# Dense stages of a graph layer: norms applied a tile later, a residual add moved to VectorE, two loads swapped, M1's first transposes before the last products

## The chip, the cores and the metric

One core of a Trainium2 chip runs the kernel. The metric is the device time of one execution in microseconds (us). Before the change the median of 3 runs is 567.51 us (563.29 to 567.92).

## The reference

A graph layer over 1250 nodes of width 512 and 20000 edges, float32 throughout:

```python
h = relu(layernorm(x))                                  # node_feats
msg = relu(h[src] + (edge_attr @ W_edge + b_edge))
aggr = segment_sum(msg, dst)
t = (1 + eps) * h + aggr
t = gelu(layer_norm(t @ W1 + b1, g1, be1))              # 512 -> 1024
t = gelu(layer_norm(t @ W2 + b2, g2, be2))              # 1024 -> 512
t = layer_norm(h + t, gA, bA)                           # "layer A"
m = gelu(t @ M1) @ M2
out = x + layer_norm(t + m, gB, bB)
```

## The kernel before

The edge part (gather, messages, scatter by one-hot products) fills some 300 us; the change does not touch it. It leaves `acc`, ten tiles of 128 nodes (NT = 10). The dense part follows. Every operand of a product is split into a high and a low float32r part, and each product is three matmuls of 128x512 (low by high, high by low, high by high), lines L1129 to L1131.

- **Stage 0** (s = 0, W1): per tile 4 transposes of the input tile on TensorE into `ps_t`, `lhs_high` (ScalarE copy, L739) and `lhs_low` (VectorE subtraction, L1001), then 24 matmuls into `ps_u`, then norm 1 and Gelu into `mid`.
- **Stage 1** (s = 1, W2): per tile 8 transposes, the same split, 24 matmuls, norm 2, Gelu, the residual row `res` (x, normalized again by ScalarE, L773) added on GpSimd (L545), and layer A's norm into `acc`.
- **M1 and M2**: `turn(2, ...)` transposes pairs of `acc` tiles (L1249), `inner(b, f, k)` is one of 8 blocks of M1's product for a batch of 4, 2 or 4 tiles (12 matmuls), `inner_values` on ScalarE applies Gelu twice (full and high part), `inner_low` on VectorE makes the low part, and `down` is M2's product.

The order is written out by hand, one program for each engine, with semaphores between them; each engine takes its instructions in order. In both stages TensorE's `step` does product(i) and then the transposes of tile i + 2. `after(s, i, p)` is the step of the other engines for tile i, whose buffers are picked by p = i mod 2. A normalization is: bias and sum (`add_product`, L1027), two tiny VectorE operations on the sum (L1030, L1031), a sum of squares on ScalarE (`variance`, L755), var + eps and its power -0.5 on GpSimd (`inv_std`, L532 and L534), then two VectorE passes: centre times gain (L1016) and scale plus shift (L1022). Layer A uses VectorE's batch-norm statistics instead (L1006, L1010) and centres in L1019. VectorE's step does it all for its own tile in one go: read the product, make the low part of tile i + 2, centre, wait for `rstd`, scale. In stage 1 it also does layer A of tile i - 1. The next weight matrix is loaded chunk by chunk in the steps of tiles 0 to 7 (`w_raw`), and split by ScalarE (`weight_high`, L750) and GpSimd (`weight_low`, L539).

TensorE reads the product buffers in turn: product(i) waits until VectorE has read product(i - 2) (`product_read`) and has made the low part of tile i (`lhs_lo_done`). In `step(1, 8)` the transposes of `acc` tiles 0 to 3 (`turn(2, 0)` and `turn(2, 1)`) come after product(1, 8); the first `inner` waits for the low parts of both. On SyncE, `load_tile(s, i + 2)` and `load_extras(s, i)` follow each other for each tile.

## Time and profile before

| | |
|---|---|
| median of 3 runs | 567.51 us (563.29 to 567.92) |
| the profiled execution | 562.67 us, of which its span 560.8 us |
| granted TensorE clock, mean of the span | 0.957 |
| busy in the span | TensorE 471.7, VectorE 407.6, ScalarE 300.4, GpSimd 325.4 us |
| W1 and W2 (stages 0 and 1) | about 301 to 437 us |
| M1 and M2 | 439 us to the end |

Busy shares are means over parts with different limits, so the stages have to be read one by one: on each engine's timeline, from the same operation of one tile to that of the next. A matmul row's duration includes its pipeline; the start-to-start distance tells the rate. A bracket at a row's end is the idle time before it and what ended it.

### The profile page before, as it was taken

Reading aid. Unit: us, or ns where it says so; the run is one execution under the profiler, and the core shown is the slowest. Engines: PE = TensorE matmul, PEld = TensorE weight load, DVE = VectorE, ACT = ScalarE, POOL = GpSimd, SP = SyncE. Lnnn points to the kernel's source line nnn. Section 1 sums busy time; section 2 is a strip of 40 time slices with the busy share of each in tenths; the row PEclk is TensorE's granted clock in tenths of the full one; section 3 lists DMA queues with packets and bytes.
Section 4 is the critical chain, followed back from the end, with each engine's and each line's share of the span. In section 5 each row is a group of like instructions: output and inputs, shape, how many; then the busy total and the mean of one; then the engine's idle time right before and its main releaser. Section 6 shows DMA issues by size and latency. Waiting matters only on the chain.

```text
span 560.8 us, 7864 instructions
## 1 busy us (share of the span) xinstructions
PE 471.7 (84%) x1915; PEld 348.7 (62%) x1916; DVE 407.6 (73%) x550; ACT 300.4 (54%) x569; POOL 325.4 (58%) x306
## 2 busy tenths in 40 slices
PE   1072999989679898898867999999998699999994
PEld 0041666656346565465546887778877589888883
DVE  7852999887379696688892888879999844472465
ACT  3742787786186786878881544455554555014000
POOL 4675788887588778888830444427777542240152
PEclk9997899989789899899989999999999799999998
DMA  8677567677667766669404522244442031121022
GB/s 279 240 210 225 181 200 233 206 220 212 192 198 209 212 203 205 193 201 348 125 1 176 207 79 79 116 151 128 148 136 76 0 97 55 39 85 29 21 92 75
DMA packets 31416, 85.26 MB, mean 152 GB/s; under 512 B 4592, under 2 KB 4928, under 8 KB 31360
## 3 DMA queue, kind: packets, MB, share of 16 engines
q0 software_dynamic: 12560, 41.17, 24.9%
q1 hardware_dynamic: 17984, 42.74, 22.2%
q10 hardware_dynamic: 816, 0.77, 0.5%
q8 instruction: 15, 0.25, 0.2%
q14 instruction: 41, 0.34, 0.2%
HBM read 72.07 MB, written 5.24 MB: 138 GB/s over the span
## 4 chain that ended last, share of the span: by engine, by line
PE 39%; DVE 24%; issue 19%; ACT 8%; POOL 4%; ACTq 3%; DMA 2%; DVEq 1%; another core or an unknown queue 1%; POOLq 0%
PE ps_t L1155 5%; DVE msg_lo L953 5%; DVE work L1022 5%; PE ps_u L1131 5%; PE ps_u L1129 5%; PE ps_u L1130 5%; PE ps_u L1139 4%; DVE z L948 4%; PE ps_t L1130 4%; PE ps_t L1131 4%; PE ps_t L1129 4%; POOL rstd L534 3%; ACTq L297 2%; ACT squares L755 2%; PE ps_t L1139 2%
## 5 line engine op out<-in xcount | busy, mean ns | idle before, releaser
L521 POOL DMA_INDIRECT rows<-gather_table,src_idx x157 | 190.6, 1214 | 60.4 <-issue 42.4
L697 ACT ACTIVATE msg_hi<-z 128x1024 fp32r<-128x1024 f32 (+1 forms) x79 | 82.8, 1048 | 67.7 <-DVE z L948 42.4
L953 DVE SCALAR_TENSOR_TENSOR msg_lo<-z,msg_hi 128x1024 fp32r<-128x1024 f32 (+1 forms) x79 | 100.8, 1277 | 0.7 <-ACT msg_hi L697 0.7
L1139 PE MATMUL ps_u<-we_raw,attr_raw 128*128 128x512 f32 x104 | 58.7, 648 | 39.7 <-issue 24.4
L532 POOL TENSOR_TENSOR var_eps<-mv,eps_t 128x1 f32<-128x1 f32 x40 | 11.5, 289 | 133.4 <-DVE mv L1010 68.4
L948 DVE TENSOR_TENSOR z<-ps_u,rows 128x1024 f32<-128x1024 f32 (+1 forms) x53 | 64.1, 1209 | 32.0 <-issue 14.7
L1129 PE MATMUL ps_u<-w_hi,lhs_lo 128*128 128x512 f32 x160 | 64.7, 405 | 4.2 <-DVE lhs_lo L1001 3.0
L1131 PE MATMUL ps_u<-w_hi,lhs_hi 128*128 128x512 f32 x160 | 62.9, 393 | 0.0
L1130 PE MATMUL ps_u<-w_lo,lhs_hi 128*128 128x512 f32 x160 | 62.8, 392 | 0.0
L1155 PE MATMUL ps_t<-msg_lo,onehot 128*128 128x512 f32 x145 | 60.7, 419 | 0.0
L1155 PE MATMUL ps_t<-msg_hi,onehot 128*128 128x512 f32 x145 | 57.7, 398 | 0.0
L1139 PEld LDWEIGHTS ps_u<-we_raw,attr_raw 128*128 128x128 f32 x104 | 20.4, 205 | 50.5 <-issue 30.5
L628 ACT ACTIVATE apart<-iota,neg_rel_last 128x128 f32<-128x128 f32 x160 | 50.6, 387 | 0.0
L1129 PE MATMUL ps_u<-we_hi,attr_lo 128*128 128x512 f32 x53 | 44.4, 837 | 0.0
L534 POOL TENSOR_TENSOR rstd<-var_eps,minus_half 128x1 f32<-128x1 f32 x40 | 40.3, 1007 | 3.1
L948 DVE TENSOR_TENSOR z<-ps_t,rows 128x1024 f32<-128x1024 f32 x26 | 31.7, 1219 | 11.7 <-PE ps_u L1131 7.1
L539 POOL TENSOR_TENSOR w_lo<-w_raw,w_hi 128x512 f32 (+1 forms) x24 | 34.6, 1444 | 8.6 <-ACT w_hi L750 8.6
L1129 PE MATMUL ps_u<-ff_in_hi,w_lo 128*128 128x512 f32 (+1 forms) x96 | 35.2, 366 | 5.0 <-DVE ff_in_lo L997 5.0
L786 ACT ACTIVATE ff_full<-ps_u 128x512 f32<-128x512 f32 (+1 forms) x24 | 12.7, 528 | 47.7 <-PE ps_u L1131 43.6
L1129 PEld LDWEIGHTS ps_u<-w_hi,lhs_lo 128*128 128x128 f32 x160 | 30.1, 188 | 11.7 <-issue 3.3
L1079 DVE TENSOR_TENSOR ff_lo<-ff_full,ff_hi 128x512 fp32r<-128x512 f32 (+2 forms) x24 | 14.7, 614 | 29.0 <-ACT ff_hi L787 29.0
L1130 PE MATMUL ps_u<-ff_in_lo,w_hi 128*128 128x512 f32 (+1 forms) x96 | 35.1, 365 | 0.0
(158 smaller groups left out, 1056.9 us busy)
## 6 DMA issues: line engine op xcount, KB each, us to landing
attr_raw<-in_attr_t SPq DMA_DIRECT2D x20, 512.0 KB
w_raw<-in_W SPq DMA_DIRECT2D x24, 256.0 KB, 2.7
tile_in<-mid SPq DMA_DIRECT2D x10, 512.0 KB, 3.3
res<-in_x SPq DMA_DIRECT2D x20, 256.0 KB, 2.7
xin<-in_x SPq DMA_DIRECT2D x5, 512.0 KB, 7.4
gather_table<-tab SPq DMA_DIRECT2D x5, 512.0 KB, 2.8
out<-work SPq DMA_DIRECT2D x10, 256.0 KB, 2.1
rows<-gather_table,src_idx POOLq DMA_INDIRECT x157
```

The costliest lines, as they stand in the source:

```text
L521: g.indirect_dma_start(rows[:, group.r, e % TPG, :], None, gather_table[:, :], bass.IndirectOffsetOnAxis(src_idx[:, e:e + 1].bitcast(u32), ...
L534: g.tensor_tensor(rstd[:, slot:slot + 1], var_eps[:, slot:slot + 1], minus_half[:, 0:1], ALU.pow).then_inc(LN[ln]["rstd"], 1)
L539: g.tensor_tensor(w_lo[1 - s % 2][:, cols], w_raw[:, p, :], w_hi[1 - s % 2][:, cols].bitcast(f32), ALU.subtract).then_inc(w_lo_done, 1)
L628: last = a.activation(apart[:, e, :], iota[:, 0:P], ACT.Square, bias=neg_rel_last[:, ds(g.gr * TPG + e, 1)])
L697: a.activation(pair(msg_hi, g, p), summed(g, p), ACT.Relu).then_inc(msg_hi_done, 1)
L948: v.tensor_tensor(summed(g, p), embedded(g, p), rows[:, g.r, 2 * p:2 * p + g.in_pair(p), :].rearrange("p a d -> p (a d)"), ALU.add).then_i ...
L953: v.scalar_tensor_tensor(pair(msg_lo, g, p), summed(g, p), 0.0, pair(msg_hi, g, p).bitcast(f32), ALU.max, ALU.subtract).then_inc(msg_lo_do ...
L1129: t.matmul(o, lhs[1][cols], rhs[0][rcols], start=first, stop=False)
L1130: t.matmul(o, lhs[0][cols], rhs[1][rcols], start=False, stop=False)
L1131: return t.matmul(o, lhs[0][cols], rhs[0][rcols], start=False, stop=last)
L1139: t.matmul(o[:, D:2 * D], attr_raw[:, g.k, (2 * p + 1) * P:(2 * p + 2) * P], we_raw[:, :], start=True, stop=True)
L1155: last = t.matmul(summed_in(bank), selection[:, e, :], m[:, g.r, e * D:(e + 1) * D], start=False, stop=(e == end and m is msg_hi), skip_gr ...
```

## The change

In stages 0 and 1 each VectorE step reads its product first and then applies the norm of the tile before it; ScalarE's Gelus move a tile later with it. Layer A's residual add goes from GpSimd to VectorE (`add_residual`), with the sum taken in the same instruction; its squares are summed on ScalarE; its norm is applied two tiles behind. GpSimd's `weight_low` waits for the norm of the tile before. SyncE sends the weight chunk ahead of the residual rows. TensorE does `turn(2, 0)` before product(1, 8) and `turn(2, 1)` before product(1, 9), and the splits of both are in step 8 of the other engines. The buffers of sums and means grow from 2 to 4 columns. The norm after M2 (layer B) keeps its code.

```diff
--- before.py
+++ after.py
@@ -432,6 +432,11 @@
             def load_extras(s, i, p):
+                if s < 3 and not (isinstance(i, int) and i >= CHUNKS):
+                    if not early(s, i):
+                        sp.wait_ge(w_lo_done, W1_CHUNKS + CHUNKS * s + i - 1)
+                    sp.dma_start(w_raw[:, p, :], A["W"][:, ds((s + 1) * WCOLS + i * D, D)]).then_inc(w_in[p], 16)
                 if s in (1, 3):
                     if not zero(i, 1):
...
                     elif s == 3:
                         sp.wait_ge(res_added, NT - 1 + i)
                     sp.dma_start(res[p][:, :], A["x"][ds(i * P, P), :]).then_inc(res_in[p], 16)
-                if s < 3 and not (isinstance(i, int) and i >= CHUNKS):
-                    if not early(s, i):
-                        sp.wait_ge(w_lo_done, W1_CHUNKS + CHUNKS * s + i - 1)
-                    sp.dma_start(w_raw[:, p, :], A["W"][:, ds((s + 1) * WCOLS + i * D, D)]).then_inc(w_in[p], 16)
@@ -528,39 +528,40 @@
             def inv_std(ln, i, slot):
-                pool.wait_ge(LN[ln]["squared" if ln in "12" else "moments"], i + 1)
+                pool.wait_ge(LN[ln]["squared" if ln in "12A" else "moments"], i + 1)
...
             def weight_low(s, i, p):
+                if s < 2 and not zero(i):
+                    pool.wait_ge(LN["12"[s]]["done"], i)
                 pool.wait_ge(w_hi_done, W1_CHUNKS + CHUNKS * s + i + 1)
...
-            def add_input(s, i, p):
-                if s == 1:
-                    pool.wait_ge(gelu2_ready, i + 1)
-                    g.tensor_tensor(work[p][:, D:H], work[p][:, D:H], res[p][:, :], ALU.add).then_inc(res_added, 1)
+            def shift_input(i, p):
...
+            def after(s, i, p):
+                weights = not (isinstance(i, int) and i >= CHUNKS)
+                if s == 0:
+                    inv_std("1", i, p)
+                    if weights:
+                        weight_low(0, i, p)
+                elif s == 1:
+                    if not zero(i, 1):
+                        inv_std("A", i - 2, 2 + p)
+                    if weights:
+                        weight_low(1, i, p)
+                    inv_std("2", i, p)
                 else:
...
-            def after(s, i, p):
-                if s < 2:
-                    inv_std("12"[s], i, p)
-                    if s == 1:
-                        if not zero(i):
-                            inv_std("A", i - 1, 3 - p)
-                        add_input(s, i, p)
-                    if not (isinstance(i, int) and i >= CHUNKS):
-                        weight_low(s, i, p)
-                else:
-                    add_input(s, i, p)
+                    shift_input(i, p)
                     inv_std("B", i, p)
...
                 if s == 1:
-                    inv_std("A", NT - 1, 3)
+                    for p in range(2):
+                        inv_std("A", NT - 2 + p, 2 + p)
...
@@ -749,30 +751,55 @@
...
-            def variance(ln, i, p, width):
+            def variance(ln, i, slot, x, width):
                 act.wait_ge(LN[ln]["mean"], i + 1)
-                a.activation(squares[:, 0:width], work[p][:, 0:width], ACT.Square, bias=neg_shift[:, p:p + 1],
-                             scale=float(width) ** -0.5, accum_out=mv[:, p, 1:2]).then_inc(LN[ln]["squared"], 1)
+                if not zero(i):
+                    act.wait_ge(LN[ln]["squared"], i)
+                elif ln != "1":
+                    act.wait_ge(LN["1"]["squared"], NT)
+                first = D if ln == "A" else 0
+                a.activation(squares[:, first:first + width], x, ACT.Square, bias=neg_shift[:, slot:slot + 1],
+                             scale=float(width) ** -0.5, accum_out=mv[:, slot, 1:2]).then_inc(LN[ln]["squared"], 1)
+            def gelu1(i, p):
+                act.wait_ge(LN["1"]["done"], i + 1)
+                a.activation(tile(mid, i), work[p][:, :], ACT.Gelu).then_inc(up_ready, 1)
+            def gelu2(i, p):
+                act.wait_ge(LN["2"]["done"], i + 1)
+                a.activation(work[p][:, D:H], work[p][:, 0:D], ACT.Gelu).then_inc(gelu2_ready, 1)
+            def input_rows(i, p):
...
+                a.activation(res[p][:, :], res[p][:, :], ACT.Relu, bias=x_nbias[:, ds(i, 1)], scale=x_rstd[:, ds(i, 1)])
             def after(s, i, p):
                 s2, i2 = ahead(s, i, p)
-                lhs_high(s2, i2, p)
-                variance("12"[s], i, p, H if s == 0 else D)
-                if not (isinstance(i, int) and i >= CHUNKS):
+                weights = not (isinstance(i, int) and i >= CHUNKS)
+                if s2 < 2 or i2 == 0:
+                    lhs_high(s2, i2, p)
+                if s == 1 and weights:
                     weight_high(s, i, p)
+                variance("12"[s], i, p, work[p][:, 0:H if s == 0 else D], H if s == 0 else D)
+                if s2 == 2 and i2 == 0:
+                    lhs_high(2, 1, 1)
                 if s == 0:
-                    act.wait_ge(LN["1"]["done"], i + 1)
-                    a.activation(tile(mid, i), work[p][:, :], ACT.Gelu).then_inc(up_ready, 1)
+                    if weights:
+                        weight_high(s, i, p)
+                    if not zero(i):
+                        gelu1(i - 1, 1 - p)
                 else:
-                    if isinstance(i, int):
-                        act.wait_ge(res_in[p], 16 * (i // 2 + 1))
+                    input_rows(i, p)
+                    if zero(i):
+                        gelu1(NT - 1, 1)
...
-                    act.wait_ge(LN["2"]["done"], i + 1)
-                    a.activation(work[p][:, D:H], work[p][:, 0:D], ACT.Gelu).then_inc(gelu2_ready, 1)
+                        gelu2(i - 1, 1 - p)
+                        variance("A", i - 1, 3 - p, work[1 - p][:, D:H], D)
@@ -787,6 +814,8 @@
...
                     weight_high(2, f, f % 2)
+                if b == 0 and f == 0:
+                    variance("A", NT - 1, 3, work[1][:, D:H], D)
...
@@ -798,6 +827,7 @@
...
                     after(s, NT - 2 + p, p)
+            gelu2(NT - 1, 1)
             lhs_high(2, 2, 0)
             inner_parts(act, 0, inner_values)
@@ -1021,56 +1051,71 @@
...
             def add_product(s, i, p, other, width):
                 dve.wait_ge(product_done, NT * s + i + 1)
                 v.scalar_tensor_tensor(work[p][:, 0:width], ps_u[p][:, 0:width], 1.0, other, ALU.mult, ALU.add,
                                        accum_out=total[:, p:p + 1]).then_inc(product_read, 1)
                 dve.wait_ge(product_read, NT * s + i + 1)
-                v.tensor_scalar(neg_shift[:, p:p + 1], total[:, p:p + 1], -float(width) ** -1.5, None, ALU.mult)
-                v.tensor_scalar(neg_mean[:, p:p + 1], total[:, p:p + 1], -1.0 / width, None, ALU.mult).then_inc(LN["12"[s]]["mean"], 1)
-            def layer_a(i, p, part):
+                mean("12"[s], p, width)
+            def norm1(i, p):
+                if zero(i):
+                    for name in ("g1", "be1"):
+                        dve.wait_ge(vec1_in[name], 16)
+                normalize("1", i, p, work[p][:, :], g1, be1, work[p][:, :]).then_inc(LN["1"]["done"], 1)
+            def norm2(i, p):
+                x = work[p][:, 0:D]
+                normalize("2", i, p, x, g2, be2, x).then_inc(LN["2"]["done"], 1)
+            def add_residual(i, p):
                 x = work[p][:, D:H]
-                if part == 0:
-                    dve.wait_ge(res_added, i + 1)
-                    moments("A", i, 2 + p, x, D)
-                else:
-                    normalize("A", i, 2 + p, x, gA, bA, tile(acc, i)).then_inc(h_ready, 1)
+                dve.wait_ge(gelu2_ready, i + 1)
+                v.scalar_tensor_tensor(x, x, 1.0, res[p][:, :], ALU.mult, ALU.add, accum_out=total[:, 2 + p:3 + p]).then_inc(res_added, 1)
+                dve.wait_ge(res_added, i + 1)
+                mean("A", 2 + p, D)
+            def norm_a(i, p):
+                normalize("A", i, 2 + p, work[p][:, D:H], gA, bA, tile(acc, i)).then_inc(h_ready, 1)
             def after(s, i, p):
-                x = work[p][:, 0:D]
                 s2, i2 = ahead(s, i, p)
-                if s2 == 2 and i2 == 1:
-                    lhs_low(s2, i2, p)
                 if s == 0:
                     if zero(i):
                         dve.wait_ge(vec1_in["b1"], 16)
                     if not zero(i, 1):
                         dve.wait_ge(up_ready, i - 1)
                     add_product(s, i, p, b1[:, :], H)
+                    if not zero(i):
+                        norm1(i - 1, 1 - p)
+                    lhs_low(s2, i2, p)
                 else:
                     if zero(i, 1):
                         dve.wait_ge(up_ready, NT - 1 + i)
                     else:
                         dve.wait_ge(gelu2_ready, i - 1)
                     add_product(s, i, p, b2[:, :], D)
-                if not (s2 == 2 and i2 == 1):
-                    lhs_low(s2, i2, p)
-                if s == 0:
+                    if s2 == 2 and i2 == 0:
+                        lhs_low(2, 0, 0)
                     if zero(i):
-                        for name in ("g1", "be1"):
-                            dve.wait_ge(vec1_in[name], 16)
-                    normalize("1", i, p, work[p][:, :], g1, be1, work[p][:, :]).then_inc(LN["1"]["done"], 1)
-                else:
+                        norm1(NT - 1, 1)
+                    else:
+                        norm2(i - 1, 1 - p)
+                    if s2 < 2:
+                        lhs_low(s2, i2, p)
+                    elif i2 == 0:
+                        lhs_low(2, 1, 1)
+                    if not zero(i, 1):
+                        norm_a(i - 2, p)
                     if not zero(i):
-                        layer_a(i - 1, 1 - p, 0)
-                    normalize("2", i, p, x, g2, be2, x).then_inc(LN["2"]["done"], 1)
-                    if not zero(i):
-                        layer_a(i - 1, 1 - p, 1)
+                        add_residual(i - 1, 1 - p)
@@ -1107,9 +1152,11 @@
-            for part in range(2):
-                layer_a(NT - 1, 1, part)
+            norm2(NT - 1, 1)
+            norm_a(NT - 2, 0)
             lhs_low(2, 2, 0)
+            add_residual(NT - 1, 1)
+            norm_a(NT - 1, 1)
@@ -1274,13 +1321,12 @@
             def step(s, i, p):
+                s2, i2 = ahead(s, i, p)
+                if s2 == 2:
+                    turn(2, i2, p)
                 product(s, i, p)
-                s2, i2 = ahead(s, i, p)
                 if s2 < 2:
                     turn(s2, i2, p)
-                elif i2 == 0:
-                    turn(2, 0, 0)
-                    turn(2, 1, 1)
```

VectorE in the loop of stage 1, one tile from the operations behind the product's read to the last pass of layer A, before:

```order
L1030 TENSOR_SCALAR neg_shift<-total 128x1 [waits product_read]
L1031 TENSOR_SCALAR neg_mean<-total 128x1
L994 REGISTER_ALU
L1001 TENSOR_TENSOR lhs_lo<-ps_t,lhs_hi 128x1024 [waits lhs_hi_done]
L1006 BN_STATS st<-work 128x6 [waits res_added]
L1010 BN_AGGR mv<-st 128x2 [waits lnA_stats]
L1014 REGISTER_ALU
L1016 SCALAR_TENSOR_TENSOR work<-work,neg_mean,g 128x512 [waits ln2_squared,ln2_mean]
L1022 SCALAR_TENSOR_TENSOR work<-work,rstd,be 128x512 [waits ln2_rstd,ln2_centered]
L1019 SCALAR_TENSOR_TENSOR work<-work,mv,gA 128x512 [waits lnA_moments]
L1022 ISA [waits lnA_rstd,lnA_centered]
L1022 SCALAR_TENSOR_TENSOR acc<-work,rstd,bA 128x512
```

and now, from the read's two small operations to the first one behind the residual add (L1061 was L1027, L1046 is the centring pass, L1052 the scaling pass, L1031 the low part):

```order
L1055 TENSOR_SCALAR neg_shift<-total 128x1 [waits product_read]
L1056 TENSOR_SCALAR neg_mean<-total 128x1
L1046 SCALAR_TENSOR_TENSOR work<-work,neg_mean,g 128x512 [waits ln2_squared,ln2_mean]
L1052 SCALAR_TENSOR_TENSOR work<-work,rstd,be 128x512 [waits ln2_rstd,ln2_centered]
L1024 REGISTER_ALU
L1031 TENSOR_TENSOR lhs_lo<-ps_t,lhs_hi 128x1024 [waits lhs_hi_done]
L1046 SCALAR_TENSOR_TENSOR work<-work,neg_mean,gA 128x512 [waits lnA_squared,lnA_mean]
L1052 ISA [waits lnA_rstd,lnA_centered]
L1052 SCALAR_TENSOR_TENSOR acc<-work,rstd,bA 128x512
L1080 SCALAR_TENSOR_TENSOR work,total<-work,res 128x512 [waits gelu2_ready]
L1055 TENSOR_SCALAR neg_shift<-total 128x1 [waits res_added]
L1056 TENSOR_SCALAR neg_mean<-total 128x1
```

The batch-norm statistics are gone; norm 2 (of tile i - 1) stands ahead of the low part, layer A (of tile i - 2) behind it, and the residual add of tile i - 1 ends the step.

ScalarE from the second split for M1 (tiles 2 and 3) on, through the step of tile 9 to the first block of M1, before:

```order
L734 ACTIVATE ff_in_hi<-ps_t 128x4x256 [waits turned]
L755 ACTIVATE squares,mv<-work,neg_shift 128x512 [waits ln2_mean]
L773 ACTIVATE res<-res,x_nbias,x_rstd 128x512 [waits res_in1]
L775 ACTIVATE work<-work 128x512 [waits ln2_done]
L734 ACTIVATE ff_in_hi<-ps_t 128x1024 [waits turned]
L786 ACTIVATE ff_full<-ps_u 128x512 [waits inner_done]
L787 ACTIVATE ff_hi<-ps_u 128x512
L750 ACTIVATE w_hi<-w_raw 128x512 [waits w_in0,product_done]
```

and now, from the squares of tile 9's product on (L736 was L734, L762 was L755, L771 was L775, L813 and L814 were L786 and L787):

```order
L762 ACTIVATE squares,mv<-work,neg_shift 128x512 [waits ln2_squared,ln2_mean]
L778 ACTIVATE res<-res,x_nbias,x_rstd 128x512 [waits res_in1]
L771 ACTIVATE work<-work 128x512 [waits ln2_done]
L762 ACTIVATE squares,mv<-work,neg_shift 128x512 [waits lnA_squared,lnA_mean]
L771 ACTIVATE work<-work 128x512 [waits ln2_done]
L736 ACTIVATE ff_in_hi<-ps_t 128x1024 [waits turned]
L813 ACTIVATE ff_full<-ps_u 128x512 [waits inner_done]
L814 ACTIVATE ff_hi<-ps_u 128x512
L752 ACTIVATE w_hi<-w_raw 128x512 [waits w_in0,product_done]
L762 ACTIVATE squares,mv<-work,neg_shift 128x512 [waits lnA_squared,lnA_mean]
L813 ACTIVATE ff_full<-ps_u 128x512 [waits inner_done]
```

Between the last product's squares and M1's first Gelu now stand two Gelus, the residual row, one layer-A sum and the third split; another layer-A sum, which waits for VectorE's add of tile 9, stands between the first and the second block.

## Rows read from the trace of the kernel before

**Rows 1.** The page's first line.
```profile
span 560.8 us, 7864 instructions
```

**Rows 2.** Busy time by stage: length, each engine's busy time, granted clock, DMA share, GB/s.
```profile
301.00:366.00 65.00, 62.30 (x288) 50.05 (x288) 47.87 (x63) 29.20 (x45) 23.30 (x24) 1.00 0.40 142
366.00:437.00 71.00, 65.58 (x328) 54.22 (x328) 64.55 (x105) 37.08 (x61) 48.54 (x55) 1.00 0.38 126
437.00:465.00 28.00, 25.99 (x111) 21.41 (x112) 17.18 (x25) 15.87 (x29) 14.24 (x15) 0.88 0.26 74
```

**Rows 3.** Timeline of TensorE, first matmuls of products: start, us, instruction, idle before.
```profile
320.03 0.48 PE L1129 MATMUL ps_u<-w_hi,lhs_lo 128*128 128x512 f32 x1
326.07 0.48 PE L1129 MATMUL ps_u<-w_hi,lhs_lo 128*128 128x512 f32 x1
...
366.67 0.47 PE L1129 MATMUL ps_u<-w_hi,lhs_lo 128*128 128x512 f32 x1 [1.22 <-issue]
...
373.04 0.48 PE L1129 MATMUL ps_u<-w_hi,lhs_lo 128*128 128x512 f32 x1
...
426.69 0.48 PE L1129 MATMUL ps_u<-w_hi,lhs_lo 128*128 128x512 f32 x1
...
439.01 0.77 PE L1129 MATMUL ps_u<-ff_in_hi,w_lo 128*128 128x512 f32 x1 [5.02 <-DVE ff_in_lo L997]
...
444.14 0.39 PE L1129 MATMUL ps_u<-ff_in_hi,w_lo 128*128 128x512 f32 x1
```

**Rows 4.** Timeline of VectorE, one tile of stage 0.
```profile
342.34 1.21 DVE L1027 SCALAR_TENSOR_TENSOR work<-ps_u,b 128x1024 f32<-128x1024 f32 x1
...
344.12 0.69 DVE L1001 TENSOR_TENSOR lhs_lo<-ps_t,lhs_hi 128x512 fp32r<-128x512 f32 x1 [0.31 <-ACT lhs_hi L739]
345.31 1.29 DVE L1016 SCALAR_TENSOR_TENSOR work<-work,neg_mean,g 128x1024 f32<-128x1024 f32 x1 [0.50 <-ACT squares L755]
347.11 2.24 DVE L1022 SCALAR_TENSOR_TENSOR work<-work,rstd,be 128x1024 f32<-128x1024 f32 x1 [0.51 <-POOL rstd L534]
```

**Rows 5.** VectorE's scaling pass of tile 8 of stage 0, where GpSimd splits no weights.
```profile
368.34 1.28 DVE L1022 SCALAR_TENSOR_TENSOR work<-work,rstd,be 128x1024 f32<-128x1024 f32 x1 [0.51 <-POOL rstd L534]
```

**Rows 6.** Timeline of GpSimd: a weight split in stage 0, then a power in stage 1.
```profile
346.98 1.29 POOL L539 TENSOR_TENSOR w_lo<-w_raw,w_hi 128x512 f32 x1
...
379.00 0.55 POOL L534 TENSOR_TENSOR rstd<-var_eps,minus_half 128x1 f32<-128x1 f32 x1
```

**Rows 7.** Timeline of VectorE in stage 1: the pass beside that power, then one tile.
```profile
379.12 0.74 DVE L1016 SCALAR_TENSOR_TENSOR work<-work,neg_mean,g 128x512 f32<-128x512 f32 x1
...
402.50 0.68 DVE L1027 SCALAR_TENSOR_TENSOR work<-ps_u,b 128x512 f32<-128x512 f32 x1
...
403.36 1.21 DVE L1001 TENSOR_TENSOR lhs_lo<-ps_t,lhs_hi 128x1024 fp32r<-128x1024 f32 x1
...
406.30 0.75 DVE L1022 SCALAR_TENSOR_TENSOR work<-work,rstd,be 128x512 f32<-128x512 f32 x1
...
407.85 1.78 DVE L1022 SCALAR_TENSOR_TENSOR acc<-work,rstd,bA 128x512 f32 x1
409.56 0.68 DVE L1027 SCALAR_TENSOR_TENSOR work<-ps_u,b 128x512 f32<-128x512 f32 x1
```

**Rows 8.** Timeline of GpSimd in the same tile.
```profile
407.79 1.29 POOL L545 TENSOR_TENSOR work<-work,res 128x512 f32<-128x512 f32 x1 [0.34 <-ACT work L775]
409.03 1.76 POOL L539 TENSOR_TENSOR w_lo<-w_raw,w_hi 128x512 f32 x1
```

**Rows 9.** ScalarE by line from 390 to 425 us: count, busy us, mean ns, idle before.
```profile
L739 ACT ACTIVATE lhs_hi<-ps_t 128x1024 fp32r<-128x1024 f32 x5 | 5.0, 1010 | 0.0
L755 ACT ACTIVATE squares<-work,neg_shift 128x512 f32<-128x512 f32 x6 | 4.4, 726 | 11.4 <-DVE neg_mean L1031 11.4
L750 ACT ACTIVATE w_hi<-w_raw 128x512 f32 x5 | 3.1, 615 | 0.0
```

**Rows 10.** DMA issues from 296 to 480 us: count, KB, median us to landing.
```profile
tile_in<-mid SPq DMA_DIRECT2D x10, 512.0 KB, 3.3
```

27 lines of the change are left out of this document (16 added, 11 removed).

## The prediction

> **What bounds the kernel now.** I read the busy time by stage first, then the timelines of TensorE, VectorE, GpSimd and ScalarE, one tile each. The change touches nothing before 301 us. In stage 0 TensorE is busy 62.3 of 65 us, in stage 1 65.6 of 71, always at the full granted clock (1.00); VectorE is the second, 64.6 of 71 us in stage 1 [rows 2]. TensorE's product starts show three rates [rows 3]. Early in stage 0 it paces itself: 326.07 - 320.03 = 6.04 us a tile. Early in stage 1, with four more transposes, 6.37 us (373.04 - 366.67), so four transposes cost 0.33 us and 24 matmuls 5.7 us, 0.238 each. Later both stages run at VectorE's pace: a step of stage 0 is 342.34 to 347.11 plus 2.16, 6.93 us [rows 4], one of stage 1 is 409.56 - 402.50 = 7.06 us [rows 7]. At the end of stage 1 TensorE stands still for 5.02 us until VectorE has made the second low part for M1, and then its first 12 matmuls take 5.13 us (439.01 to 444.14) where 12 x 0.238 = 2.86 is the usual [rows 3]; the granted clock of that stretch is 0.88, a part of it at 1.2 GHz instead of 2.4 [rows 2].
>
> **Why VectorE is slow in stage 0.** Each step waits for ScalarE's squares (0.50) and for `rstd` (0.51), and the last pass takes 2.24 us while GpSimd splits weights for 1.29 us (346.98 to 348.27) [rows 4, 6]; without that split it takes 1.28 [rows 5]. In stage 1 the same happens to layer A's pass: 1.78 us beside GpSimd's residual add of 1.29, against 0.75 for an equal pass [rows 7, 8]. VectorE passes that read PSUM do not stretch: 0.68 and 1.21 us beside the splits [rows 7, 8].
>
> **Stage 0, the change's cost.** Norm 1 of tile i - 1 follows the read of product i, so both waits (squares, `rstd`) lie a whole tile back and go. The split of weights waits for the norm and then falls beside the low part, which reads PSUM. VectorE's step becomes 1.47 (read and two small operations, 344.12 - 0.31 - 342.34) + 1.29 + 1.28 + 0.69 = 4.7 us, under TensorE's 6.04. If the split still meets a pass it is 5.7, still covered. The cover of ScalarE is large too (29.2 us busy of 65 [rows 2]). TensorE then paces all ten tiles: product 9 starts at 320.03 + 6 x 6.04 + 0.33 = 356.6, the first product of stage 1 at 356.6 + 6.37 = 363.0 instead of 366.67 [rows 3]: **-3.7 us**.
>
> **Stage 1.** VectorE's step is now read 0.86 (403.36 - 402.50), norm 2 0.75 + 0.75, low part 1.21, norm A 0.75 + 0.75, residual add with its sum and two small operations [rows 7]. The add has no row. Its bounds are 0.68, the sum-taking pass from PSUM [rows 7], and 1.78, a pass of two SBUF operands in GpSimd's way; I take 0.75, an uncontended pass of this size, plus 0.18 for the small operations (0.86 - 0.68), since GpSimd has no wide work left at the step's end. The statistics and their wait go, and GpSimd's residual add (1.29 [rows 8]) goes with its collision. Sum: 6.0. GpSimd's split moves: from a product's end, transposes 0.7, ScalarE's copy 1.01, weights' high part 0.62 [rows 9], GpSimd 1.29, hand-overs about 0.4 (one is 0.34 [rows 8]): it ends at 4.0, and VectorE comes to norm A at 3.6. That is a wait of 0.4: 6.4 us, as durations overlap a little 6.2 to 6.4. TensorE needs 6.37. So the stage goes from VectorE's pace to TensorE's, with nothing to spare, but VectorE may be late: the low part of tile i + 2, made at 3.6 us, is wanted at 6.4 + 0.7, so 3.5 us of lateness cost nothing.
>
> A loop runs through three engines, because ScalarE's squares for layer A wait for the residual add and stand ahead of its next copy: squares 0.73 + 0.19, copy 1.01, high weights 0.62, split 1.29, then VectorE's rest of norm A about 0.55 + 0.75 and the add 0.93, hand-overs 0.3: 6.4 us again, no worse than TensorE.
>
> Product 9 starts at 363.0 + 9 x 6.37 + 0.7 (one more set of transposes ahead of product 8) = 421.0, instead of 426.69: **another -2.0**. The queues that are moved past: on SyncE the residual rows of tile i now wait for VectorE's add of tile i - 2, at the end of step i - 1, and `tile_in` for tile i + 3 stands behind them. It is issued some 0.6 us after the add, lands 3.3 us later [rows 10] and is wanted 6.5 us after it: 2.6 us to spare. The weights are ahead of that wait, wanted more than a tile later, and cost nothing.
>
> **The seam to M1.** Both pairs of `acc` are transposed before product 9 and both low parts made in step 8, which makes that VectorE step 7.2 us (0.86 + 2 x 1.21 + 4 x 0.75 + 0.93), 0.8 over, inside the 3.5. The first block of M1 follows product 9 and the third set of transposes: 421.0 + 6.37 = 427.4 instead of 439.01: **-5.9 more, -11.6 in all**. With no idle time ahead of it I expect the clock to stay, so 5.13 becomes 2.86: **-2.3**.
>
> What is late next is the queue behind product 9. VectorE reads it at 427.3 and then has norms 2 of tiles 8 and 9, norms A of 7, 8 and 9, the adds of 8 and 9 and the third low part before the first low part of M1. ScalarE waits about 2 us for tile 9's residual rows (issued after the add of tile 7). I follow it to the first high part of M1 at 436.4, the second at 439.4, the third at 442.5 and the fourth at 446.0. TensorE wants them at its blocks 4 to 7, 427.4 + 4 x 2.86 = 438.8, then 441.7, 444.6 and 447.4. Slack is 2.4, 2.3, 2.1 and 1.4 us: cost nothing, thinly. From the second batch on, all moves as one piece.
>
> **Sum:** 3.7 + 2.0 + 5.9 + 2.3 = 13.9 us. The profiled execution took 562.67 us (span 560.8 [rows 1] and 1.9 around it); it would take 548.8. The median of before, 567.51, lies 4.8 above that execution, so the median forecast is 567.5 - 13.9 = **553.6 us**; a median that falls on the lower kind of run would be near 549.
>
> **Rivals.**
> *A, VectorE keeps stage 1* (14%). Its step is 7.0, as now, if the add costs 1.3 to 1.8 or norm A meets the whole split. For: 6.4 against 6.37 is no margin, and 1.78 has been seen [rows 7]. Then 10 x 0.65 = 6.5 us late at step 9. TensorE lets 3.5 of it pass, loses 3.0, and the high parts of M1, 6.5 late on a chain with 1.4 to 2.4 of slack, take the loss to about 5.5: 567.5 - 8.4 = 559.1.
>
> *B, small GpSimd operations block VectorE* (6%). In the trace a power ran from 379.00 to 379.55 and the centring pass that began at 379.12 took 0.74, no longer than others [rows 6, 7]; that speaks against. If they did block, two powers in a step add 2 x 0.55 = 1.1 us: 7.5 a step, 11 late, 7.5 lost at the last product and 2 more in the queue behind it: 567.5 - 4.4 = 563.1. The Trainium skill has the rule ("SBUF — State Buffer", Who interferes with whom): a VectorE instruction with two SBUF inputs and a GpSimd instruction that reads SBUF exclude each other, for the whole of the first. For the wide operations the rows agree with it; for the power row they do not.
>
> *C, slower: M1's first batch starves* (4%). ScalarE's sum for tile 9 stands between block 0 and block 1, low parts behind norm A of tile 9, weight chunk 2 behind GpSimd's split of chunk 0, which is behind the same norm. Three waits in a row, and after each long one TensorE may run 12 matmuls at 1.2 GHz again, 2.3 us [rows 3]. It decides against the change once the fourth high part comes later than 447.4 + 13.9 = 461 us; at 467, 573 us. For: it is the longest queue that the change makes. Against: it would have to be 15 us longer than I count.
>
> *D, the seam stays* (4%): M1's start is held by something that the rows do not show, and only stages 0 and 1 gain: 567.5 - 5.7 = 561.8.
>
> **Numbers.** The forecast with its own spread, 548 to 556, holds 70%; A 14%, B 6%, C 4%, D 4%, and 2% lie below 548. A measurement of this kernel tells about 1% from no change, so 561.8 and 573.2 are the bounds. Faster by over 1%: forecast, A and below, 0.86. Same: B and D, 0.10. Slower: C, 0.04. The range reaches from 548 (562.7 - 13.9, rounded down) over A and most of the add's bounds to 561.
>
> **What would show it.** TensorE's starts 6.04 apart through stage 0 and 6.37 through stage 1; VectorE's scaling pass of stage 0 at 1.28 instead of 2.24; no wait ahead of the first product of stage 1; M1's first block right behind the transposes, at a granted clock of 1.00; ScalarE's first high part of M1 some 9 us behind that block's start, with no TensorE wait at blocks 4 to 7. I am wrong if the product starts of stage 1 drift to 7 us, or if TensorE waits for ScalarE within M1's first batch.

## The result, and the profile after

The changed kernel takes 556.51 us (median of 4 runs, 554.97 to 558.24) against 565.4 us for the kernel before (4 runs, 563.03 to 567.92): a ratio of 0.9849, interval 0.9807 to 0.9892. It is faster by 1.5%, 8.5 us on the 565.4 of the new comparison: the interval leaves out both no change and a gain of 2%. The forecast was 13.9 us off 567.5, 553.6 us with a range of 548 to 561; its own case was to lie between 548 and 556. The profiled execution took 554.97 us, 7.7 less than that of before.

The page's first line of the profile after, against [rows 1]:

```profile
span 553.2 us, 7925 instructions
```

Busy time by stage after the change, for stage 0, stage 1 and the seam, and M1 until M2's first matmul (columns: length; busy time of TensorE's matmuls, its weight loads, VectorE, ScalarE and GpSimd; granted clock; DMA share; GB/s):

```profile
303.70:366.30 62.60, 62.60 (x288) 50.82 (x289) 39.77 (x63) 30.84 (x44) 24.81 (x26) 0.98 0.40 142
366.30:430.70 64.40, 64.40 (x332) 54.25 (x330) 56.31 (x114) 40.65 (x72) 31.09 (x42) 1.00 0.39 127
430.70:468.80 38.10, 35.68 (x212) 31.13 (x210) 25.87 (x44) 24.72 (x52) 17.84 (x17) 1.00 0.26 77
```

In the first two rows TensorE's busy time equals the length of the stage: it never stands still, where 2.7 and 5.4 us were idle in [rows 2]. In the third it is busy 35.68 of 38.10. Of the three stretches this is the one where the change left idle time, and where the forecast failed.

TensorE's timeline after the change, the marks that answer to [rows 3] and the two waits of the third stretch (start, us, instruction, idle before it and what ended it):

```profile
303.68 0.76 PE L1176 MATMUL ps_u<-w_hi,lhs_lo 128*128 128x512 f32 x1 [1.07 <-DVE lhs_lo L1031]
305.09 0.63 PE L1176 MATMUL ps_u<-w_hi,lhs_lo 128*128 128x512 f32 x1
...
311.10 0.48 PE L1176 MATMUL ps_u<-w_hi,lhs_lo 128*128 128x512 f32 x1
317.14 0.48 PE L1176 MATMUL ps_u<-w_hi,lhs_lo 128*128 128x512 f32 x1
...
366.32 0.48 PE L1176 MATMUL ps_u<-w_hi,lhs_lo 128*128 128x512 f32 x1
372.66 0.47 PE L1176 MATMUL ps_u<-w_hi,lhs_lo 128*128 128x512 f32 x1
...
424.34 0.48 PE L1176 MATMUL ps_u<-w_hi,lhs_lo 128*128 128x512 f32 x1
430.68 0.47 PE L1176 MATMUL ps_u<-ff_in_hi,w_lo 128*128 128x512 f32 x1
...
448.31 0.50 PE L1176 MATMUL ps_u<-ff_in_hi,w_lo 128*128 128x512 f32 x1 [0.90 <-ACT ff_hi L814]
...
463.01 0.39 PE L1176 MATMUL ps_u<-ff_in_hi,w_lo 128*128 128x256 f32 x1 [1.52 <-ACT ff_hi L814]
```

The reader sees 6.04 us a tile in stage 0 (311.10 to 317.14), 6.34 in stage 1 (366.32 to 372.66) and still that between its last product and M1 (424.34 to 430.68), with nothing waited for at the seam. Two waits for ScalarE's high part stand in M1. At the top, product 0 of stage 0 takes 7.42 us to the next start; its first matmuls last 0.63 instead of 0.40.

From such marks the dense part can be laid out as a ledger. It begins at the second product of stage 0, so that the edge part and that slow first product stay out of it; each figure is the distance from one mark to the next, in us. "Batch 0" runs from M1's first block to the transposes of batch 1, "batch 1" from there to M2's first matmul.

| profiled execution | stage 0 | stage 1 | seam | batch 0 | batch 1 | sum |
|---|---|---|---|---|---|---|
| before | 58.72 | 60.02 | 12.32 | 24.37 | 13.05 | 168.48 |
| after | 55.22 | 58.02 | 6.34 | 23.24 | 14.84 | 157.66 |
| difference | -3.50 | -2.00 | -5.98 | -1.13 | +1.79 | -10.82 |

From M2's first matmul to the end both take the same (84.4 us). The profiled difference is 7.6 us and not 10.8, since the first product of stage 0 starts 1.76 us later (303.68 against 301.92) and takes 1.39 us more (7.42 against 6.03). Whether these 3.15 us belong to the change was open, and was the first thing to ask.

VectorE's timeline after the change, one step of stage 0 and one of stage 1, against [rows 4, 7]:

```profile
342.54 1.28 DVE L1046 SCALAR_TENSOR_TENSOR work<-work,neg_mean,g 128x1024 f32<-128x1024 f32 x1
343.85 1.28 DVE L1052 SCALAR_TENSOR_TENSOR work<-work,rstd,be 128x1024 f32<-128x1024 f32 x1
...
347.18 1.22 DVE L1061 SCALAR_TENSOR_TENSOR work<-ps_u,b 128x1024 f32<-128x1024 f32 x1 [1.44 <-PE ps_u L1178]
...
384.77 0.69 DVE L1061 SCALAR_TENSOR_TENSOR work<-ps_u,b 128x512 f32<-128x512 f32 x1 [1.01 <-PE ps_u L1178]
...
388.22 1.09 DVE L1046 SCALAR_TENSOR_TENSOR work<-work,neg_mean,gA 128x512 f32<-128x512 f32 x1
389.49 0.75 DVE L1052 SCALAR_TENSOR_TENSOR acc<-work,rstd,bA 128x512 f32 x1 [0.18 <-DVE work L1046]
390.16 0.68 DVE L1080 SCALAR_TENSOR_TENSOR work<-work,res 128x512 f32<-128x512 f32 x1
```

The scaling pass of stage 0 is back at 1.28 us, both waits within the norm are gone, and VectorE now waits 1.44 us for TensorE: the bound has changed sides. In stage 1 the residual add took 0.68 us, the lower of its two bounds; layer A's centring pass is the one stretched (1.09), by the rest of GpSimd's weight split.

The end of the queue behind the last product: ScalarE, GpSimd and VectorE in M1's batch 0 after the change, in order of time:

```profile
439.49 0.60 ACT L814 ACTIVATE ff_hi<-ps_u 128x512 fp32r<-128x512 f32 x1
...
442.68 0.59 ACT L814 ACTIVATE ff_hi<-ps_u 128x512 fp32r<-128x512 f32 x1
...
443.53 3.00 POOL L541 TENSOR_TENSOR w_lo<-w_raw,w_hi 128x512 f32 x2
443.67 1.71 DVE L1052 SCALAR_TENSOR_TENSOR acc<-work,rstd,bA 128x512 f32<-128x512 f32 x1 [0.51 <-POOL rstd L534]
445.30 2.38 DVE L1124 TENSOR_TENSOR ff_lo<-ff_full,ff_hi 128x512 fp32r<-128x512 f32 x2
447.17 0.60 ACT L813 ACTIVATE ff_full<-ps_u 128x512 f32<-128x512 f32 x1 [3.38 <-DVE ff_lo L1124]
447.66 0.59 ACT L814 ACTIVATE ff_hi<-ps_u 128x512 fp32r<-128x512 f32 x1
...
449.14 0.61 ACT L814 ACTIVATE ff_hi<-ps_u 128x512 fp32r<-128x512 f32 x1
...
453.21 0.63 ACT L752 ACTIVATE w_hi<-w_raw 128x512 fp32r<-128x512 f32 x1 [1.97 <-DMA w_raw<-in_W]
...
458.13 0.63 ACT L752 ACTIVATE w_hi<-w_raw 128x512 fp32r<-128x512 f32 x1 [1.66 <-DMA w_raw<-in_W]
```

The first four high parts (L814) end 9.4, 12.6, 17.6 and 19.1 us behind the block start at 430.68; the forecast had 9.0, 12.0, 15.1 and 18.6. The third has jumped: ScalarE waits 3.38 us for VectorE's first low part, and VectorE is held by GpSimd's first two splits of M2's weights: its scaling pass takes 1.71 instead of 0.75, and two low parts 2.38 instead of 1.4. Behind that, ScalarE waits for the weight chunks themselves (1.97 and 1.66 us), because a chunk is loaded into one of two buffers only when its predecessor there has been split. GpSimd's first split of M2's weights starts 12.9 us behind M1's first block (443.53), in the kernel before 8.4 us (447.40 behind 439.01).

### The profile page after: what moved, and what is told of

Its sections match the earlier page's. It is cut to its first block, busy times and chain, and to the rows that moved or that the text cites. A ratio compares the mean times of both kernels' runs of the same rounds, so it can differ in the third digit from the quotient of the medians.

```text
span 553.2 us, 7925 instructions
## 1 busy us (share of the span) xinstructions
PE 466.0 (84%) x1915; PEld 345.9 (63%) x1916; DVE 394.2 (71%) x570; ACT 308.3 (56%) x589; POOL 314.5 (57%) x296
## 4 chain that ended last, share of the span: by engine, by line
PE 59%; DVE 14%; issue 11%; ACT 4%; another core or an unknown queue 4%; DMA 2%; ACTq 2%; POOL 2%; DVEq 0%; POOLq 0%; SPq 0%
PE ps_t L1202 9%; PE ps_u L1176 9%; PE ps_u L1177 9%; PE ps_u L1178 9%; PE ps_u L1186 5%; PE ps_t L1177 4%; PE ps_t L1178 4%; PE ps_t L1176 4%; DVE msg_lo L983 3%; DVE z L978 3%; PE ps_t L1186 3%; PE ps_t L1306 2%; PE ps_t L1195 2%; ACT apart L630 1%
## 5 line engine op out<-in xcount | busy, mean ns | idle before, releaser
L532 POOL TENSOR_TENSOR var_eps<-mv,eps_t 128x1 f32<-128x1 f32 x40 | 21.5, 537 | 133.6 <-ACT squares L762 72.5
L1186 PE MATMUL ps_u<-we_raw,attr_raw 128*128 128x512 f32 x104 | 56.9, 629 | 41.2 <-DVE attr_lo L989 36.8
L541 POOL TENSOR_TENSOR w_lo<-w_raw,w_hi 128x512 f32 (+1 forms) x24 | 32.7, 1364 | 18.3 <-ACT w_hi L752 13.6
L1061 DVE SCALAR_TENSOR_TENSOR work<-ps_u,b 128x1024 f32<-128x1024 f32 (+1 forms) x20 | 19.1, 956 | 27.2 <-PE ps_u L1178 26.6
L762 ACT ACTIVATE squares<-work,neg_shift 128x512 f32<-128x512 f32 (+1 forms) x30 | 25.9, 863 | 22.3 <-DVE neg_mean L1056 22.3
L813 ACT ACTIVATE ff_full<-ps_u 128x512 f32<-128x512 f32 (+1 forms) x24 | 12.6, 525 | 41.2 <-PE ps_u L1178 35.2
L1178 PEld LDWEIGHTS ps_u<-w_hi,lhs_hi 128*128 128x128 f32 x160 | 30.3, 189 | 7.0
```

The source lines that it names most:

```text
L541: g.tensor_tensor(w_lo[1 - s % 2][:, cols], w_raw[:, p, :], w_hi[1 - s % 2][:, cols].bitcast(f32), ALU.subtract).then_inc(w_lo_done, 1)
L762: a.activation(squares[:, first:first + width], x, ACT.Square, bias=neg_shift[:, slot:slot + 1], scale=float(width) ** -0.5, accum_out=mv[ ...
L1178: return t.matmul(o, lhs[0][cols], rhs[0][rcols], start=False, stop=last)
L1186: t.matmul(o[:, D:2 * D], attr_raw[:, g.k, (2 * p + 1) * P:(2 * p + 2) * P], we_raw[:, :], start=True, stop=True)
```

## The experiments

All kernels below are the change with the edit that is named. In these runs, on four chips, the edge part was shorter (product 0 of stage 0 starts at 288 to 295 us instead of 302 and 304), and the kernel before took 554.4 to 558.4 us; ratios and the ledger carry over, absolute times do not. A ledger is read from one profiled execution of each kernel; stages that an edit does not touch come out the same within 0.2 us from kernel to kernel.

**The change itself, once more.** No edit.

> The changed kernel once more, unaltered. Theory Q (queue): the dense part, from the second product of stage 0 to M2's first matmul, is 157.7 us again, within 0.3, because nothing in it depends on chance; it holds the 0.9 us wait before M1's seventh block and about 2 us lost in M1's second batch. The 3.2 us by which this part began later than in the kernel before (1.8 in the edge part, 1.4 of slow first matmuls) is chance, so here it is another number, between -3 and +4. Rival E (edge): moving instructions cost the edge part something steady, then the second product of stage 0 starts at 311 us again, 3 us later than before, and not at 308.

Measured: 542.99 us (542.37 to 546.93, 6 runs), before 554.38 (552.53 to 559.07, 11 runs), ratio 0.9804 (0.9761 to 0.9847). The ledger is 55.22, 58.02, 6.36, 23.13, 14.78, sum 157.51: stage by stage the first one, within 0.15 us. Product 0 of stage 0 took 6.03 us this time, so the 1.39 us of slow matmuls are chance. The other 1.76 us, the later start, can't be read off this run, as the kernel before was not profiled on this chip. Two numbers speak for chance there too: on this one chip four kernels with the same edge part began product 0 between 290.21 and 293.58 us, and the whole time fell by 10.9 us (1 - 0.9804 of 554.38, by the interval 8.5 to 13.2), where the ledger has 11.0. So the change is worth about 11 us, and the shortfall against 13.9 sits in M1's two batches.

**M2's first two weight chunks ahead of M1.** Loads, high parts (ScalarE) and low parts (GpSimd) of chunks 0 and 1 move before M1's first high part, so that the later ones run two ahead; GpSimd also waits for layer A's norms of tiles 8 and 9 (`h_ready`) ahead of its further splits. The diff shows GpSimd, then ScalarE in step 8 of stage 1 and in batch 0.

```diff
+                    if isinstance(i, int) and i == NT - 2:
+                        weight_low(2, 0, 0)
...
-                    for p in range(2):
-                        inv_std("A", NT - 2 + p, 2 + p)
-                    with pool.Fori(0, CHUNKS // 2) as j:
+                    inv_std("A", NT - 2, 2)
+                    pool.wait_ge(h_ready, NT - 1)
+                    weight_low(2, 1, 1)
+                    inv_std("A", NT - 1, 3)
+                    pool.wait_ge(h_ready, NT)
+                    with pool.Fori(1, CHUNKS // 2) as j:
...
+                            weight_high(2, 0, 0)
+                            weight_high(2, 1, 1)
...
-                if b == 0:
-                    weight_high(2, f, f % 2)
+                if b == 0 and f < CHUNKS - 2:
+                    weight_high(2, f + 2, f % 2)
```

> M2's first two weight chunks are loaded ahead of residual rows 8 and 9, and split in the steps of tiles 8 and 9; GpSimd's further splits wait for layer A's norms. Theory Q: the ScalarE queue of M1's first batch is freed of the chunk loads, so the 0.9 us wait and the 2.0 us in the second batch go: dense part 157.7 - 2.9 = 154.8 us, time 0.5% under the changed kernel. Rival S (splits collide): the early splits push VectorE's norms of tiles 8 and 9 back by over 2 us and M1 waits for its high parts all the same: 157 to 159 us.

Measured: 541.59 us (539.39 to 544.05, 6 runs), ratio 0.9762 (0.9718 to 0.9806). Ledger 55.23, 58.01, 6.34, 23.04, 13.57, sum 156.19, where 154.8 was expected: 1.3 us gained in the ledger, and as much left (the two whole times have intervals that overlap). The collision had only been moved. ScalarE, GpSimd and VectorE in batch 0 of this kernel:

```profile
431.23 4.10 DVE L1134 TENSOR_TENSOR ff_lo<-ff_full,ff_hi 128x512 fp32r<-128x512 f32 x3
431.66 3.12 POOL L543 TENSOR_TENSOR w_lo<-w_raw,w_hi 128x512 f32 x2 [1.20 <-DVE acc L1062]
...
435.86 0.63 ACT L759 ACTIVATE w_hi<-w_raw 128x512 fp32r<-128x512 f32 x1 [2.77 <-DMA w_raw<-in_W]
```

Chunks 2 and 3 are still split back to back beside VectorE's low parts (three in 4.10 us), and chunk 4, whose load waits for the first of them (the two buffers), makes ScalarE wait 2.77 us.

**GpSimd's splits wait for the last norm A.** This takes away the collision with the norm, and delays the chunk loop.

```diff
+                    pool.wait_ge(h_ready, NT)
                     with pool.Fori(0, CHUNKS // 2) as j:
                         for p in range(2):
                             weight_low(2, 2 * j + p, p)
```

> The changed kernel with one more wait: GpSimd splits no M2 chunk until layer A's last norm is applied. Theory Q has two causes in M1's first batch: (P) GpSimd's two splits stand in the way of VectorE's last norm (1.71 instead of 0.75 us) and first low part (1.7 instead of 0.7), which makes the third high part late; (D) the loop of load, high part, low part of the chunks, two buffers, about 5 us for two chunks, keeps ScalarE behind. If P alone made the 0.9 us wait, it goes here and the third high part comes about 1 to 1.5 us sooner; D then stays or grows: ScalarE waits for chunks 2 to 7 as before and the second batch still loses 2 us or 1 more: dense part 156.8 to 158.5. If D made both, the 0.9 us wait stays.

Measured (one run): 544.86 us, ledger 55.23, 58.01, 6.34, 23.04, 16.38, sum 159.00, above the 156.8 to 158.5 expected. The third high part ends 15.7 us behind the block start instead of 17.5, and the wait of 0.79 at the seventh block is gone: that wait was the collision's. But the loop of load, high part and low part over two buffers now starts later still (14.2 us behind M1's first block instead of 12.7). It brings a wait of 0.70 one block later, so that batch 0 hardly moves, and waits of 0.83 and 1.96 us in batch 1, which gets 1.6 us longer. So the late loop alone makes waits in both batches, and a later one makes longer ones. That it, and not the collision, is the larger part of the change's loss is likely from this, but no run takes away the late loop and leaves the collision.

**The splits ahead and spread out.** As the edit before last, but GpSimd splits chunk 2 ahead of layer A's last power and only chunk 3 behind the last norm, and ScalarE's high parts stand so that no two loads wait together.

```diff
                     weight_low(2, 1, 1)
+                    weight_low(2, 2, 0)
                     inv_std("A", NT - 1, 3)
                     pool.wait_ge(h_ready, NT)
-                    with pool.Fori(1, CHUNKS // 2) as j:
+                    weight_low(2, 3, 1)
+                    with pool.Fori(2, CHUNKS // 2) as j:
...
-                if b == 0 and f < CHUNKS - 2:
-                    weight_high(2, f + 2, f % 2)
+                if b == 0 and f in (0, 1, 3, 4, 6, 7):
+                    c = {0: 2, 1: 3, 3: 4, 4: 5, 6: 6, 7: 7}[f]
+                    weight_high(2, c, c % 2)
```

> Like m2_early, with chunks 4 to 7 split by ScalarE behind M1's blocks 3, 4, 6 and 7 instead of 2 to 5, and chunk 2 split by GpSimd ahead of layer A's last power. In m2_early ScalarE stood 2.77 us in front of chunk 4, whose load cannot begin before chunk 2 is split, and the next high part stood behind it; the dense part took 156.2 us. Theory Q: the wait at block 7 (0.69) and in the second batch (0.26) go, dense part 154.7 to 155.3 us. Rival: the splits of chunks 6 and 7 now end late and M1's second batch pays for them: 156 or more.

Measured: 540.95 us (535.86 to 542.84, 6 runs), before 554.67 (551.45 to 558.5, 17 runs), ratio 0.9729 (0.9678 to 0.978). Ledger 55.21, 58.02, 6.36, 22.08, 13.05, sum 154.72. Busy time of its batch 0 and of its batch 1:

```profile
420.00:443.00 23.00, 23.00 (x107) 18.99 (x106) 18.74 (x35) 16.58 (x33) 14.54 (x14) 1.00 0.26 70
443.00:456.00 13.00, 13.00 (x113) 13.00 (x112) 6.15 (x10) 8.39 (x20) 3.84 (x3) 1.00 0.19 59
```

TensorE is busy 23.00 of 23.00 and 13.00 of 13.00 us. With the queue out of the way the sum is 13.8 us under the kernel before, the forecast's 13.9: what the forecast expected of these two batches can be had, but only with M2's weights split earlier than in the change. It is the fastest kernel of the study by its median and its ratio, though its interval still touches that of the change; what separates them is the 2.8 us of the ledger.

**The second pair of `acc` back where it was.** Transposes of tiles 2 and 3 behind product 8 and not ahead of product 9, their low part at the head of VectorE's last step (TensorE, then VectorE); all else as in the change.

```diff
                 product(s, i, p)
                 if s2 < 2:
                     turn(s2, i2, p)
+                elif i2 == 0:
+                    turn(2, 0, 0)
+                    turn(2, 1, 1)
...
+                    if s2 == 2 and i2 == 1:
+                        lhs_low(2, 1, 1)
```

> The changed kernel with the seam undone: both pairs of layer A's tiles are transposed after product 8 and the second low part is made at the start of step 9, as before. Theory (the forecast's): M1's first block waits again for the second low part, 3 to 5 us of TensorE idle, its first 12 matmuls take about 5 us instead of 2.8, and in return the high parts of M1 come in time, so that the 2.9 us of the two batches go: dense part 157.7 + 5 + 2.3 - 2.9, 161 to 163 us. Rival: VectorE is ahead of TensorE now, so that the second low part is ready anyway and the seam edit is worth under 1 us: 158 to 159.

Measured (one run): 546.23 us, ledger 55.22, 58.01, 9.00, 23.58, 13.91, sum 159.72: 2.2 us more than the change, where 3.5 to 5.5 were expected. TensorE waits 2.41 us for the second low part, not 5.02 as before, and M1's first 12 matmuls take 4.35 us (about 5 were expected, 2.84 in `again`). So of the 6.0 us at the seam, 2.7 come from the early transposes, and 3.3 from VectorE no longer being late when it comes to them. The 2.7 in turn are paid back in part: batch 1 is 0.9 us shorter, and batch 0, whose start is 1.5 us slower, has no wait at its seventh block and is only 0.4 us longer.

**The residual add back on GpSimd,** at the end of its step, with layer A's statistics on VectorE (GpSimd's `after`, then VectorE's `add_residual`).

```diff
+                    if not zero(i):
+                        add_input(i - 1, 1 - p)
...
-                v.scalar_tensor_tensor(x, x, 1.0, res[p][:, :], ALU.mult, ALU.add, accum_out=total[:, 2 + p:3 + p]).then_inc(res_added, 1)
                 dve.wait_ge(res_added, i + 1)
-                mean("A", 2 + p, D)
+                moments("A", i, 2 + p, x, D)
```

> The changed kernel with layer A's residual add back on GpSimd and its batch-norm statistics back on VectorE; all norms stay a tile behind. The forecast's accounting: the add (1.29 us) can begin only behind GpSimd's split and norm 2's power, at about 5 us of the step, and meets VectorE's norm A; VectorE then waits for it and does statistics of 0.68 + 0.18: a step of 7.2 to 7.8 us instead of 6.4, of which 3.5 us of lateness are free. The nine products of stage 1 take 58.0 now and 61 to 65 here; the dense part 157.5 + 5 to 10. Rival N (the residual move is worth nothing, all gain comes from the norms): 58 to 59 us, dense part under 159.

Measured: 554.85 us (550.79 to 560.66, 10 runs), ratio 0.9995 (0.996 to 1.0031): of the whole time no gain is seen. Ledger 55.23, 62.48, 8.02, 25.82, 14.87, sum 166.42, of which 2.1 us under the kernel before; stage 0 keeps its 3.5. VectorE's step in stage 1 becomes 7.75 us (mean of steps 2 to 8), more than the 7.05 of before. VectorE in that kernel, the end of one step and the head of the next, and GpSimd in the latter:

```profile
395.51 0.69 DVE L1040 BATCH_NORM_STATS2 st<-work 128x6 f32<-128x512 f32 x1 [1.18 <-POOL work L546]
...
396.48 0.69 DVE L1065 SCALAR_TENSOR_TENSOR work<-ps_u,b 128x512 f32<-128x512 f32 x1
...
399.20 1.30 POOL L541 TENSOR_TENSOR w_lo<-w_raw,w_hi 128x512 f32 x1 [1.76 <-DVE work L1056]
...
401.17 0.55 POOL L534 TENSOR_TENSOR rstd<-var_eps,minus_half 128x1 f32<-128x1 f32 x1
401.69 1.41 POOL L546 TENSOR_TENSOR work<-work,res 128x512 f32<-128x512 f32 x1
```

Each step now goes round VectorE's norm, GpSimd's split, power and add, and VectorE's statistics, which wait 1.18 us for the add. So in stage 1 the norms a tile later are worth nothing with the add in this place; the step is even 0.7 us longer than before. Two things were not tried: the add ahead of the split, where the kernel before has it, and this kernel without the split's wait for norm 2, which is a link of this round (the 1.76 us in the row above).

**One pass more on VectorE.** A second 128x512 pass of two SBUF operands (it leaves its data as they are), behind the wait for the Gelu and ahead of the add.

```diff
+                v.scalar_tensor_tensor(res[p][:, :], x, 0.0, res[p][:, :], ALU.mult, ALU.add).then_inc(again, 1)
+                dve.wait_ge(again, i + 1)
                 v.scalar_tensor_tensor(x, x, 1.0, res[p][:, :], ALU.mult, ALU.add, accum_out=total[:, 2 + p:3 + p]).then_inc(res_added, 1)
```

> The changed kernel with one pass more on VectorE in each step of stage 1, ahead of the residual add: residual rows plus 0 times the Gelu, 128x512, the same values, about 0.8 us with its wait. It tests how late VectorE may be. The forecast's accounting: a step of 7.2 us, 5 to 6 us late at product 8, of which 3.5 us are free: the nine products take 60 us instead of 58.0, M1's first block then waits 2 to 3 us for the second low part, and the high parts come 6 us late: dense part 162 to 167 us instead of 157.5. Rival T (VectorE and TensorE are in step, nothing is free): nine products take 58 + 7 = 65 us and more.

Measured (one run): 551.56 us, ledger 55.22, 59.73, 7.30, 26.94, 15.09, sum 164.28. VectorE's step is 7.14 us. 0.69 us a tile make ten times that, 6.8 us in all, but only 1.7 of it show in stage 1; the rest arrives in the seam (0.9), in batch 0 (3.8) and in batch 1 (0.3). Stage 1 and the sum came as expected; the wait ahead of M1's first block was 0.72 us, not 2 to 3. TensorE's transposes late in this kernel's stage 1:

```profile
400.37 1.09 PE L1309 MATMUL ps_t<-ident,tile_in 128*128 128x128 f32 x8 [0.72 <-DMA tile_in<-mid]
407.51 1.10 PE L1309 MATMUL ps_t<-ident,tile_in 128*128 128x128 f32 x8 [0.57 <-DMA tile_in<-mid]
```

It is not a low part that TensorE waits for first but its input tile: on SyncE that load stands behind the residual rows, which wait for VectorE's add. At the first of these waits VectorE is 2.3 us late: its add ends at 395.48, and it reads product 5 at 395.66, where the product ended at 393.32. The tile is issued at 396.64, 1.2 us behind the add (forecast 0.6), and lands at 400.33, 3.7 us after that (forecast 3.3). Of the 2.3 us TensorE feels 0.72: some 1.6 us of lateness are free on this path, not the 3.5 that the forecast counted for the low part, nor its 2.6 for this queue. `rows_first`, below, gives 1.5 (1.70 us late, 0.23 us waited).

**Residual rows ahead of the weights again,** SyncE's old order.

```diff
-                if s < 3 and not (isinstance(i, int) and i >= CHUNKS):
-                    if not early(s, i):
-                        sp.wait_ge(w_lo_done, W1_CHUNKS + CHUNKS * s + i - 1)
-                    sp.dma_start(w_raw[:, p, :], A["W"][:, ds((s + 1) * WCOLS + i * D, D)]).then_inc(w_in[p], 16)
...
                     sp.dma_start(res[p][:, :], A["x"][ds(i * P, P), :]).then_inc(res_in[p], 16)
+                if s < 3 and not (isinstance(i, int) and i >= CHUNKS):
+                    if not early(s, i):
+                        sp.wait_ge(w_lo_done, W1_CHUNKS + CHUNKS * s + i - 1)
+                    sp.dma_start(w_raw[:, p, :], A["W"][:, ds((s + 1) * WCOLS + i * D, D)]).then_inc(w_in[p], 16)
```

> The changed kernel with the two loads swapped back: residual rows first. They wait for VectorE's add of tile i - 2, at the start of step i, and the weight chunk stands behind them: it lands about 2.9 us into the step where ScalarE wants it at 1.9. My accounting: ScalarE, GpSimd's split and with it VectorE's norm A come 1 us later, VectorE's step goes from 6.45 to about 7.2, and the nine products of stage 1 from 58.0 to 59.5 to 62 us. Rival: ScalarE's slack takes it in, 58.0.

Measured (one run): 547.69 us, ledger 55.23, 58.94, 7.03, 26.20, 13.62, sum 161.02, 3.5 us over the change; stage 1 alone is below what was expected. VectorE's step is 6.97 us. One step of ScalarE, GpSimd and VectorE:

```profile
398.32 0.63 ACT L752 ACTIVATE w_hi<-w_raw 128x512 f32 x1 [1.58 <-DMA w_raw<-in_W]
...
399.14 1.27 POOL L541 TENSOR_TENSOR w_lo<-w_raw,w_hi 128x512 f32 x1 [1.47 <-ACT w_hi L752]
399.20 1.77 DVE L1052 SCALAR_TENSOR_TENSOR acc<-work,rstd,bA 128x512 f32 x1
```

The weights now wait for VectorE's add, ScalarE waits 1.58 us for them, and GpSimd's split, so much later, falls on layer A's scaling pass: 1.77 instead of 0.75. The swap of two loads, which the forecast priced at nothing, carries a third of the gain (3.5 of 11.0 us, each ledger from one execution).

**GpSimd's split without its wait for the norm.**

```diff
-                if s < 2 and not zero(i):
-                    pool.wait_ge(LN["12"[s]]["done"], i)
```

> The change, but GpSimd's split of the weights no longer waits for the norm of the tile before, in either stage. The forecast's step for stage 0: if the split meets a pass of VectorE, that step is 5.7 us instead of 4.7 and still under TensorE's 6.04, so the stage stays at 6.04 a tile (first to last mark 55.2 us, as in the change) although VectorE's wide passes are stretched. Stage 1: the split then stands about 1.2 us earlier in each step, where VectorE is in norm 2 instead of at norm A, so VectorE's norm A should be back near 0.75 and one pass of norm 2 be stretched instead: the step stays between 6.2 and 6.7 us, and the marks of stage 1 within 1 us of 58.02. Rival (the wait is needed): the split delays norm 2, norm 2 delays the Gelu, the residual add and the squares, and stage 1 takes 60 us or more.

Measured (one run): 542.98 us, ledger 55.22, 58.01, 6.35, 22.65, 14.89, sum 157.12. No stage differs by more than 0.6 us, but not for the expected reason: in stage 0, and in most steps of stage 1, the split does not move. GpSimd in one such step of stage 1:

```profile
394.12 1.07 POOL L534 TENSOR_TENSOR rstd<-var_eps,minus_half 128x1 f32<-128x1 f32 x1
395.16 1.31 POOL L539 TENSOR_TENSOR w_lo<-w_raw,w_hi 128x512 f32 x1
```

It stands right behind layer A's power, which VectorE's norm 2 stretches from 0.55 to 1.07 us. There the collision of the two engines orders them by itself. In the steps of tiles 4 and 6 the split does begin sooner (2.30 us behind VectorE's read instead of 2.67), and layer A's centring pass is back at 0.74 us, as was expected; VectorE's step stays 6.51 us in the mean. It comes to product 9 some 0.4 us sooner, and batch 0 is 0.5 us shorter. The added wait is not needed.

**Two more powers of one column on GpSimd in each step of stage 1.**

```diff
                     inv_std("2", i, p)
+                    for k in (p, 2 + p):
+                        g.tensor_tensor(spare[:, k:k + 1], eps_t[:, 0:1], minus_half[:, 0:1], ALU.pow)
```

> The change with two more powers of one column (0.55 us each) on GpSimd in every step of stage 1, written to a spare buffer. Case B of the forecast (a small GpSimd operation that reads SBUF holds up a VectorE pass of two SBUF inputs) gives up to 1.1 us more in each VectorE step, 7.5 us: product starts drift off 6.37, the marks of stage 1 take 60 us or more and the dense part 160 or more. My theory: small operations cost VectorE nothing, and they themselves are what waits (one in the change took 1.09 us beside a VectorE pass, 0.55 else); VectorE's step stays 6.45, stage 1 58.0 and the dense part 157.5 to 158.

Measured (one run): 543.53 us, stage 1 57.94, sum 157.79, VectorE's step 6.50 us as in the change (6.51). GpSimd and VectorE in one step:

```profile
390.58 0.75 DVE L1055 SCALAR_TENSOR_TENSOR acc<-work,rstd,bA 128x512 f32 x1 [0.16 <-DVE work L1049]
391.06 1.28 POOL L565 TENSOR_TENSOR spare<-eps_t,minus_half 128x1 f32<-128x1 f32 x2
391.25 0.68 DVE L1083 SCALAR_TENSOR_TENSOR work<-work,res 128x512 f32<-128x512 f32 x1
```

Two powers ran beside two passes of VectorE, and the passes kept 0.75 and 0.68 us. In this run's trace 33 passes of 128x512 with two SBUF operands began while a one-column operation of GpSimd was running and no wide one, and none took more than 0.75 us. Case B is refuted.

**A longer idle time at the seam.** `seam_back` with four, then with seven VectorE passes of 128x512 ahead of the second low part.

```diff
                     if s2 == 2 and i2 == 1:
+                        for k in range(4):
+                            v.scalar_tensor_tensor(ff_full[1][:, :], g2[:, :], 1.0, g2[:, :], ALU.mult, ALU.add).then_inc(passed, 1)
+                            dve.wait_ge(passed, k + 1)
                         lhs_low(2, 1, 1)
```

> seam_back (the second pair of transposes and low parts for M1 where they stood before the change) with four extra VectorE passes of 128x512 ahead of the second low part, so that TensorE stands still longer ahead of M1's first block: 2.41 us of wait become 4.6 to 5.3. If it is the idle time that cost the kernel before its 2.3 us (granted clock 0.88 there), M1's first 12 matmuls take about 5.1 us again instead of 2.8, and the seam takes 11.3 to 12. Rival (the slow matmuls at M1's start came from something else, for instance from the code that ran before them): they take 2.8 us although TensorE has waited about 5.

> seam_idle with seven extra passes instead of four. Four made the wait ahead of M1's first block 3.44 us (2.41 without them, since part of them fell into time that VectorE had free), and M1's first 12 matmuls still took 2.8 us, so that idle time cost no clock. Three more passes of 0.72 should make the wait 5.5 us, a little more than the 5.02 us that stood there before the change. My theory, that the idle time was what lowered the granted clock there: the first 12 matmuls take about 5.1 us again, and the seam 14.5 us (10.02 + 2.15 + 2.3). Rival (the fall at that place was of another cause, such as the stretch of work ahead of it): they take 2.8 us, and the seam 12.2.

Measured (one run each): with four passes TensorE waited 3.44 us, less than expected, and lost no clock (547.4 us; seam 10.02, batch 0 22.31, sum 160.49). With seven it waited 5.61 us (543.79 us; seam 12.19, batch 0 24.73, batch 1 13.06, sum 163.23). TensorE at M1's start, with four and with seven:

```profile
423.62 0.47 PE L1177 MATMUL ps_u<-ff_in_hi,w_lo 128*128 128x512 f32 x1 [3.44 <-DVE ff_in_lo L1025]
423.94 0.39 PE L1178 MATMUL ps_u<-ff_in_lo,w_hi 128*128 128x512 f32 x1
```

```profile
419.69 0.77 PE L1177 MATMUL ps_u<-ff_in_hi,w_lo 128*128 128x512 f32 x1 [5.61 <-DVE ff_in_lo L1025]
420.25 0.63 PE L1178 MATMUL ps_u<-ff_in_lo,w_hi 128*128 128x512 f32 x1
...
424.95 0.62 PE L1177 MATMUL ps_u<-ff_in_hi,w_lo 128*128 128x512 f32 x1
```

Twelve matmuls take 5.26 us (419.69 to 424.95) after the long wait, at a granted clock of 0.50, the 1.2 GHz level, and 2.84 (423.62 to 426.46) after the shorter. Batch 0 is 2.4 us longer, the forecast's term for the clock. The expectation had put that cost into the seam; it falls behind its end mark, in batch 0, so 12.2 + 2.4 is what was expected as 14.5.

## Why the prediction was right, and where it was not

The measured 556.51 lies 2.9 us above the forecast, inside the range of 548 to 561 but 0.5 above the spread of 548 to 556 that the forecast gave its own case. One of its two signs of being wrong came: TensorE waits for ScalarE within M1's first batch (0.90 us at the seventh block). Its mechanism holds in the four terms of the sum and fails in one that it put at nothing. There is some luck in the 2.9: the median of the kernel before was 567.5 when the forecast was made and 565.4 in the comparison. By its steps:

- **Stage 0, -3.7.** Measured -3.50. TensorE paces all ten tiles at 6.04 us. VectorE's step is shorter than that, as counted; the split comes behind the low part, not beside it, since `var_eps` ahead of it takes 1.21 us beside VectorE's scaling pass. No run undoes the move of the norms by itself; that it makes this gain is read from the rows of the two kernels.
- **Stage 1, -2.0.** Measured -2.00. VectorE starts its steps 6.51 us apart (mean, from the read of tile 2 to that of tile 8), over the 6.2 to 6.4 of the forecast and over TensorE's 6.34. So it falls behind, and reads product 9 at 431.23, 1.2 us after its end; the free lateness takes that in, and the pace is TensorE's. The step has the parts that were counted: the add 0.68 (forecast 0.75), and norm A's centring 0.3 to 0.4 us longer than alone (forecast a wait of 0.4). Case A (14%) did not come, but it was close: `extra_pass` shows that 0.69 us more a step cost 6.8 us, and that only some 1.6 us of lateness are free.
- **The seam, -5.9.** Measured -5.98. `seam_back` divides it: 2.7 from the early transposes, 3.3 from the shorter steps ahead of them. Case D did not come.
- **The clock, -2.3.** The first 12 matmuls of M1 run at the granted clock of 1.00. `seam_idle7` brings back the idle time and the 2.4 us with it, though `seam_idle` and `seam_back` show that the length of the wait alone does not decide (last section).
- **The queue behind product 9, "cost nothing, thinly".** This step failed. It cost 3.0 us: batch 0 should have been 24.37 - 2.3 = 22.07 and was 23.24, batch 1 should have stayed at 13.05 and was 14.84. The forecast followed ScalarE's high parts and let GpSimd's splits of M2's weights pass as harmless, though [rows 4, 6] and [rows 7, 8] had shown what a wide GpSimd operation does to a VectorE pass. They collide with the last norm A and the first low parts, which moves the third high part from 15.1 to 17.6 us behind the block's start, past its 17.2 (`split_waits`, without the collision: 15.7). And "from the second batch on, all moves as one piece" forgot that the weight chunks come through a loop over two buffers, which begins only behind GpSimd's power for the last norm: counted from M1's start it begins 4.5 us later than before (12.9 against 8.4). `m2_spread` takes both away and finds the forecast's sum, 13.8 us; how the 3.0 us divide between the two is not shown.
- **The loads on SyncE, "cost nothing".** True of the new order, but the old one costs 3.5 us with the other edits in place. The swap is a part of the gain that the forecast did not name.
- **Case B** is refuted by `small_powers`. By the Trainium skill's rule ("SBUF — State Buffer", Who interferes with whom) whichever of the two begins first holds the other up. Where VectorE is first the rows agree: a power takes 1.07 instead of 0.55 us. Where a small GpSimd operation is first they do not: the pass keeps its 0.75 us. Where a wide one is first they agree again: 0.75 becomes 1.71 to 1.78.
- **Case C** named the right place, M1's first batch; the loss there was a seventh of its price.

Against the forecast's 13.9 us the ledger has 10.8 to 11.0, and the repeated comparison 10.9. The first comparison showed 8.5; its profiled execution had 3.15 us of slow first product and late start, the first shown to be chance by `again`, the second likely so. How much of them stood in its other runs is not known, and the two intervals overlap.

## What to carry to other kernels

When a change moves work away from the engine that sets the pace, follow the queue to the next stage with every engine that writes the same memory, and its buffers: lateness that a stage lets pass is paid in the next one (5.1 of the 6.8 us of `extra_pass`). A wide GpSimd operation is priced by what VectorE does beside it, so place it where VectorE reads PSUM or waits. Of a bundle of edits, ask what each is worth without the others: the norms a tile later gave nothing in stage 1 with the residual add at the end of GpSimd's step, and the order of two loads was worth 3.5 us.

## What the runs showed that was not expected

- Idle time alone does not tell whether TensorE's clock falls. After 5.02 and 5.61 us of waiting the first 12 matmuls took 5.13 and 5.26 us; after 3.44 us they took 2.84; but after 2.41 us, in `seam_back`, 4.35, with the granted clock at 0.72 in the 6 us around it:

```profile
421.00:427.00 6.00, 4.49 (x13) 3.63 (x14) 5.72 (x14) 2.18 (x5) 1.60 (x3) 0.72 0.30 101
```

- At the start of stage 0, behind two waits of 1.03 and 1.07 us (1.84 and 1.07 in the kernel before), the first product took 6.03 us in some profiled executions (before, `again`, `m2_spread` and six more) and 7.42 to 7.59 in others (after, `m2_early`, `seam_back`, `extra_pass`, `small_powers`): 1.4 to 1.6 us that come and go with 7 to 9 matmuls near its start that last 0.6 us or more instead of 0.39.
- A GpSimd operation on one column, 0.19 us for the addition alone, took 1.21 us beside a VectorE pass of 1.28 in stage 0 of the change, from 343.98 to the pass's end.
